# A transformer block with a sparse expert layer: the drain of the attention loop reordered, scatters in gated groups, 39 expert blocks in place of 43

## What is computed

```python
ln2 = layer_norm(h1, ln2_weight, ln2_bias)        # 8192 tokens of 256
probs = softmax(ln2 @ router_weight)              # 8 experts
top_p, top_i = top_k(probs, 2)
top_p = top_p / sum(top_p)
# sorted by expert; each expert keeps its first cap = 2560 tokens
fc1 = gelu(einsum('ech,ehf->ecf', xt, moe_w1))    # 256 -> 512
fc2 = einsum('ecf,efh->ech', fc1, moe_w2)         # 512 -> 256
out = h1 + scatter_add(padded_tid, fc2 * padded_probs)
```

## Time and profile before

| | us |
|---|---|
| median of 3 runs | 1218.48 |
| lowest, highest | 1216.59, 1225.96 |
| the profiled execution | 1220.39 |
| its span, first to last instruction | 1218.6 |

### The profile page before, as it was taken

One profiled execution on the slowest core, in us unless ns is written; L12 is line 12 of the kernel. 1 busy time (PEld: TensorE's weight loads), 2 busy tenths in 40 slices (PEclk: granted clock), 3 DMA queues, 4 the chain that ended last, 5 costly groups with the idle time before them and its releaser, 6 DMA issues. The chain is left out here.

```text
span 1218.6 us, 25497 instructions
## 1 busy us (share of the span) xinstructions
PE 1120.3 (92%) x8218; PEld 1022.2 (84%) x8249; DVE 921.7 (76%) x2282; ACT 834.2 (68%) x1927; POOL 585.9 (48%) x564
## 2 busy tenths in 40 slices
PE   7899999999998899999987974989999999999994
PEld 4699999999997688788776863788999999999984
DVE  5677777776775689888888863897778888888872
ACT  2467666667665698888886872666676778778771
POOL 0012122121212244888887776377656546556545
PEclk9899999999998899999998996899999999999997
DMA  9524344353321032444444454378878778887853
GB/s 311 127 91 140 100 142 130 108 164 108 114 71 54 22 100 79 128 137 133 132 132 133 129 178 161 112 184 199 191 178 187 194 185 210 209 195 194 206 140 53
DMA packets 119056, 175.47 MB, mean 144 GB/s; under 512 B 13776, under 2 KB 88944, under 8 KB 118896
## 3 DMA queue, kind: packets, MB, share of 16 engines
q1 hardware_dynamic: 92336, 139.63, 37.7%
q0 software_dynamic: 26592, 34.24, 15.1%
HBM read 107.96 MB, written 67.69 MB: 144 GB/s over the span
## 5 line engine op out<-in xcount | busy, mean ns | idle before, releaser
L1268 POOL DMA_INDIRECT out_rows<-y,row x142 | 238.9, 1683 | 196.6 <-DVE y L1869 75.9
L178 PE MATMUL gh<-w2h,hh 128*128 128x256 f32 x568 | 160.8, 283 | 1.1 <-DVE y L1869 1.1
L180 PE MATMUL gh<-w2h,hl 128*128 128x256 f32 x568 | 160.7, 283 | 0.0
L179 PE MATMUL gh<-w2l,hh 128*128 128x256 f32 x568 | 160.7, 283 | 0.0
L1800 DVE TENSOR_TENSOR hl<-h,hh 128x512 fp32r<-128x512 f32 (+1 forms) x172 | 100.9, 596 | 67.1 <-ACT h L1483 62.1
L1246 POOL DMA_INDIRECT slot_rows<-kept,slot x112 | 117.9, 1053 | 32.8 <-issue 29.5
L1482 ACT ACTIVATE hh<-gw 128x512 fp32r<-128x512 f32 (+1 forms) x86 | 45.7, 531 | 107.6 <-issue 98.0
L178 PEld LDWEIGHTS gh<-w2h,hh 128*128 128x128 f32 x568 | 108.9, 192 | 2.2 <-issue 1.2
L179 PEld LDWEIGHTS gh<-w2l,hh 128*128 128x128 f32 x568 | 108.9, 192 | 1.0
L180 PEld LDWEIGHTS gh<-w2h,hl 128*128 128x128 f32 x568 | 108.9, 192 | 0.0
L819 POOL TENSOR_SCALAR spread<-mv 128x2 f32<-128x2 f32 x32 | 7.1, 221 | 211.6 <-DVE mv L967 211.2
(11 more groups left out here) (322 smaller groups left out, 3955.2 us busy)
## 6 DMA issues: line engine op xcount, KB each, us to landing
w1e<-in_moe_w SPq DMA_DIRECT2D x43, 512.0 KB
w2e<-in_moe_w SPq DMA_DIRECT2D x43, 512.0 KB
x_rows<-x SPq DMA_DIRECT2D x64, 256.0 KB, 2.4
xg<-x_rows SPq DMA_DIRECT2D x64, 256.0 KB
xr<-slot_rows SPq DMA_DIRECT2D x28, 532.0 KB
xT<-in_xT SPq DMA_DIRECT2D x32, 256.0 KB, 2.7
x<-in_x SPq DMA_DIRECT2D x32, 256.0 KB, 3.8
out_rows<-res SPq DMA_DIRECT2D x64, 128.0 KB
```

Of the source, the lines that this page charges most:

```text
L178: nc.tensor.matmul(out, at_a(ah), at_b(bh), start=first, stop=False, skip_group_check=True)
L179: nc.tensor.matmul(out, at_a(ah), at_b(bl), start=False, stop=False, skip_group_check=True)
L180: return nc.tensor.matmul(out, at_a(al), at_b(bh), start=False, stop=last, skip_group_check=True)
L1268: g.indirect_dma_start(out=out, out_offset=bass.IndirectOffsetOnAxis(ap=row[m % NR][:, t:t + 1], axis=0), in_=y[m % 2][:, t, :], in_offset ...
```

## The change

- *Last rows.* The rows of the last pair are loaded into the key buffers `kvd` (`last12`, `load_last`), once its value transposes are done, and no longer into `xg` after the previous `res`.
- *Order of the drain.* TensorE turns block 1 at k = 33 and computes hidden slice 0 of block 0 between the last turn and the last logits (k = 34), the other three behind the logits. The recount waits for `summed`, the sums of VectorE, and stands ahead of layer one of block 1; it writes to the banks `gs`. The turn of block 2 lies between the halves of layer two of block 0. On ScalarE `features(1)`, the high part of `w2` and the first gelu come ahead of the last ranks; the last batch's Exp comes behind the gelus of block 0. On VectorE `w1_rest(0)` stands ahead of the last but one `shift`, `x_rest(0)` behind the last, `x_rest(1)` ahead of `w1_rest(1)`, `h_rest(0)` ahead of the scan. The wait for the scatters of batch 5 moves from ScalarE's `gelu` to VectorE's `h_rest` (the tiles `hh0` and `hl0` change places).
- *Scatters.* Those due at k = 31 and later come two steps later; the second half of batch 6 joins `place_late` (`LATE` = 12 groups). At k = 34, 35 and 36 GpSimd first waits for the last logits, the last choice and the recount.
- *Filler matmuls* (`busy`, and six in `step(1)`) write results that nothing reads.
- *Blocks.* `FULLS` = 32, so 7 halves and 39 blocks; `late_table` and `owners` now also let a full block that is left over take a single unit.
- *Tile signals.* `y_did` counts tiles; GpSimd waits per tile, TensorE's layer two waits for the banks of its own half.

```diff
-FULLS = 28
+FULLS = 32
...
-LATE = 2 * BATCHES[-1][1]
+LATE = 2 * BATCHES[-1][1] + BATCHES[LATE_BATCH][1]
...
 opening, TensorE:
+            def busy(n):
+                for _ in range(n):
+                    t.matmul(pa[0][:], pr.identb[:], pr.causalb[:].rearrange("p t g s -> p (t g s)"), start=True, stop=True)
...
+                if k == I1 + 1:
+                    busy(9)
                 if has(k - 2):
                     for u in places:
                         after(pe, act_did["nrm"], k - 2, u)
...
+                if k == I1 + 1:
+                    busy(4)
                 if has(k - 2):
                     for u in places:
                         after(pe, dve_did["nT"], k - 2, u)
...
             pipeline(step, -2, I1 + 2)
+            busy(8)
...
 rows_and_experts:
+        last12 = [a[:].rearrange("p t g s -> p (t g s)").rearrange("p (k n) -> p k n", k=2) for a in kvd]
+        rows12 = lambda j, u: last12[u] if j == LAST else x12[u][:]
...
-                for part in range(n):
-                    if k == first + n + DEPTH + 2 + part:
+                for part in range(n if m != LATE_BATCH else n // 2):
+                    due = first + n + DEPTH + 2 + part
+                    if k == (due if due < I2 - 1 else due + 2):
...
+            def load_last(u):
+                after(sp, pe_did["vT"], LAST, u)
+                sp.dma_start(last12[u].rearrange("p k n -> p (k n)"),
+                             src[bass.ds(group(LAST, u), 1)].rearrange("a p n -> (a p) n")).then_inc(x_last[u], 16)
...
             step(EARLY_STORES + 2)
+            for u in places:
+                load_last(u)
             pr.fetch_x(sp, 1)
...
 GpSimd:
+                if k == I2 + 2:
+                    after(pool, act_did["logit"], LAST, U2 - 1)
+                if k == I2 + 3:
+                    pool.wait_ge(chosen_did, len(BATCHES))
+                if k == I2 + 4:
+                    pool.wait_ge(recounted, 1)
...
-                pool.wait_ge(y_did, m + 1)
                 for t in range(SIZE[m] // P):
+                    pool.wait_ge(y_did, DONE[m] + t + 1)
...
-                for j in range(min(2 * m, m + 2), min(2 * m + 2, m + 3, LATE)):
+                for j in range(min(2 * m, m + LATE - BATCH), min(2 * m + 2, m + LATE - BATCH + 1, LATE)):
                     place_late(j)
...
 TensorE:
+                if k == 1:
+                    for _ in range(6):
+                        t_.matmul(ps_h[0][:], pr.identb[:], pr.causalb[:].rearrange("p t g s -> p (t g s)"),
+                                  start=True, stop=True)
...
                 if k == I2 + 1:
-                    layer1(0, range(0, U2))
+                    turn_block(1)
                 if k == I2 + 2:
-                    layer1(0, range(U2, FC))
-                    turn_block(1)
+                    layer1(0, range(1, FC))
 
             pipeline(pe, step, then)
+            pe.wait_ge(summed, 1)
+            pe.wait_ge(xh_did, 2)
...
+            layer1(1)
             pe.wait_ge(rank_out, len(BATCHES))
             pe.wait_ge(totalled, 1)
...
+            layer2(0, range(0, TB // 2))
+            pe.wait_ge(limit_in, 1)
             turn_block(2)
-            layer1(1)
-            layer2(0, range(0, TB // 2))
+            layer2(0, range(TB // 2, TB))
...
 VectorE:
-                ins.then_inc(y_did, 1)
+                                        None, ALU.mult).then_inc(y_did, 1)
```

138 lines of the change are left out of this document (80 added, 58 removed).

## The result

The changed kernel takes 1215.5 us (median of 22 runs) beside 1220.9 for the kernel before on the same chip: ratio 0.9948, 95% interval 0.9924 to 0.9972. It is faster by 0.5% (6.3 us by the ratio, 5.4 by the medians), not by the 24 us of the forecast (1196). On two chips where the kernel before takes 1208 us, the ratio is 1.0021 (1.0001 to 1.0042) and 0.9999 (0.9971 to 1.0027): there the change is worth nothing or costs a little. The profiled execution of the changed kernel is one of its slower ones, 1224.1 us (span 1222.0).

What follows compares the result with a forecast made beforehand. TensorE, busy 92% of the span, was taken as the bound, short of work at two handovers, with the tail third. From 1220.4 us, minus 19 (drain), 2 (fillers), 1.5 (blocks) and 1.5 (tile signals) gave 1196; 8-in-10 range 1189 to 1209.

Steps and rivals of the forecast that it cites:

- the late groups: Four more groups of rows move into the expert loop; the forecast's sum has no term for their cost.
- the hold of 9.9 us: In the drain, TensorE's signals reached other engines about 9.9 us late beside 16 scatters; if held again, the drain saves 9.9.
- Drain, minus 19: From attention loop to expert loop: layer two of block 1 starts at 768.2, not 788.03; 19 us taken, bounds 9.9 and 21.2.
- Fillers, minus 2: 27 filler matmuls in TensorE's waits where the opening meets the attention loop: gain 2 us, between a loss of 6.7 and gain of 4.
- 39 blocks, minus 1.5: Expert loop: four blocks of 512 rows replace eight of 256, saving 1.5 us, between 0.5 and 2.
- Tile signals, minus 1.5: Each y tile releases its own scatter, so trains start 1.2 us sooner: 1.5 us of the tail, between 0 and 3.
- The slower rival: GpSimd falls behind in the expert loop through late scatters, a debt of 25 us: 1209, or 1233 with slower landings; chance 0.05.
- its clause on the landing: Against the slower rival: the 11.3 us per block contain a landing wait, so part of the late scatters' 5.2 us is free.
- the y buffers forgive one block: In the slower rival: y buffers absorb 12 us of GpSimd's debt; the other 13 stop VectorE's scaling, then TensorE.
- Signals held again: Rival: in the drain TensorE's signals are held again, at the counts; all 9.9 us return, giving 1206; chance 0.17.
- Clock at 1.2 GHz through the drain: Rival: TensorE's matmuls in the drain stay at 1.2 GHz, 12.7 us more, some 4 of it in waits: 1205; chance 0.14.
- my limit of 780: Sign in the new profile: the forecast is wrong if layer two of block 1 starts after 780.

Runs made afterwards that it cites:

- after_2: The changed kernel run again without an edit, on chip D, where the kernel before takes 1207.8 us: 1208.5 us, ratio 0.9999 to the kernel before.
- best_2: The changed kernel without filler matmuls and with the scatters of the kernel before (16 in the drain, no gates, 8 late groups), chip D: 1201.6 us, ratio 0.9942.

## Why the prediction was wrong

Three steps failed on chip A, where the forecast was made: the late groups were put at nothing (they cost 4 us in the tail and some before it), the fillers got the wrong sign (plus 2.5 us for minus 2), and the 3 us given back behind the drain are in no term. On other chips a fourth step failed: the hold of 9.9 us, half of the term for the drain, was taken as the kernel's own.

- **Drain, minus 19: right in order, 2 us short, and not for every chip.** Choice at +14.7 (forecast 738.2, which is +12.6), recount +21.4 (+18.4 to +21.4), layer two of block 1 +45.7 (+42.6). The terms by waits and matmuls held. But 9.9 of the 19 were a hold seen in one execution. I wrote that only one execution was in evidence and drew no case from it in which the kernel before has no hold; that case costs half the term (8.7 saved on B), and on B the profile shows it. It would not have saved the forecast on chip A, where the hold is there.
- **What comes after the drain: missing from the sum.** Of the 16.8 us, 3 are given back by the y of block 1, where the turn of block 4 waits 2.05 us for its rows.
- **Fillers, minus 2: wrong sign.** Measured plus 1.9 to 2.6, in eight of nine profiles. The trace gave both bounds and I took the middle of a gain, reading the stretch at 1.2 GHz as something that gaps cause and fillers remove. They moved it into denser work. The Trainium skill (page "TensorE: Matmul & The Clock Gate", section "Part 4: PE-mode transpose") says that transposes don't count as activity for the clock as matmuls do. These runs neither show nor refute that; the gain near 4 that I worked out by it did not come.
- **39 blocks, minus 1.5: right sign, too small** (3.5).
- **Tile signals, minus 1.5: right**, 1.3 in the tail.
- **The late groups: put at nothing, cost 4 us in the tail and 0, or 3 to 8, before it.** The tail is after_2 against best_2, the rest the stage of the experts in the three profiles where the early lag stayed. The slower rival (GpSimd behind in the expert loop, 0.05) names the engine, with a price of 13 us or 37, but not the cause. The debt that it counts up from the late scatters' own time comes to 4 to 6 us at block 4 and is mostly paid back, as its clause on the landing says. What GpSimd cannot pay back is a stop of 4 to 5 us that the change pushed into a train. The profile before has that stop at 1041.97 (4.37 us, between two blocks) and a second of 2.54 us at 1205.49, which is inside the 11.3 us that I read as a block's period; I passed over both. My clause "the y buffers forgive one block" was right: TensorE waits 2.3 us for y, and the rest is paid at the end, where nothing forgives.
- **Signals held again:** no remote wait over 2.0 us in the changed kernel's profiles. **Clock at 1.2 GHz through the drain:** in part (744.0 to 754.2, the first 7 us of layer one), inside the 2 to 3 us that the drain fell short.

Of the signs that I named, layer two of block 1 starts at 782.59, behind my limit of 780, but only because this execution's loop was 12 us longer; TensorE does not wait for y in the first eight blocks.

On chip A the stages add up so, leaving out the loop but for the fillers: drain -16.8, experts +4.6 (3 given back, 3.5 saved by the blocks, the rest the late groups), tail +4.3, fillers +2.5: -5.4 us, and 6.3 was measured. On B: -8.7, +7.3, +4.0 and +1.9, together +4.5, beside a measured +2.5 (0.1 to 5.1). That is one profile for each kernel and chip, and the stage of the experts varies by 8 us between profiles of the changed kernel, so the agreement is better than it deserves.

## What to carry to other kernels

A wait that one profile shows as "remote" may belong to the chip: take it as a case of its own, with a forecast for both, and profile the kernel before a second time before building on it. An engine with 1.5 us of slack in 12 cannot pay back a single stop of 5 us, so before giving it more work look in its timeline for stops that hide in its idle time, ask where the new work will push them, and look at what is queued behind its last piece on other engines. And fillers that lift the granted clock in one window have to be judged by the step times behind it, since the slow stretch may only move.

## What was not expected of the hardware

- The same kernel takes 1220 us on some chips and 1208 on others, and between the profiles on A and B 10 of the 12 us are one wait: TensorE's signals reach ScalarE and VectorE 8 to 10 us late beside a train of 16 scatters.
- GpSimd stops with its inputs ready or nearly so for 4.1 to 5.8 us, after the 212th, 220th or 224th transfer by the pattern of the program, in all 18 profiles 60 scatter-adds behind the last row scatter.
- The wait for the landing of a block's last scatter-add, 3.0 to 3.5 us in the quiet parts, is mostly 4.5 to 6.3 where it falls among the next block's loads (in the first profile after the change the last add of a block ends at 894.11, three loads are issued from 893.80 on, and the wait is 4.61). A train that ends just before those loads therefore starts its successor late, and GpSimd keeps its lag instead of recovering it (6.2 us from block 4 to 10 in the first profile).
